# One copy for the values, and ScalarE for some normalisations, in an attention and feed-forward layer on eight cores

## The chip, the cores and the metric

The kernel runs on the 8 cores of one Trainium2 chip. Each core computes one of the 8 sequences of the batch by itself, with no exchange between cores, so all cores run the same program on data of the same size. The time is the device time of the slowest core, in microseconds (us). Engines are named as the profile names them: PE is TensorE (PEld its loads of the stationary operand), DVE VectorE, ACT ScalarE, POOL GpSimd, SP SyncE.

## What is computed

One transformer layer with normalisation behind each part, on x of shape (8, 2048, 1024), with 16 heads of 64. The attention weights are the second-order polynomial 1 + s + s*s/2 in place of an exponential, causal, divided by their sum. The second matmul takes its input as integers, scaled by the largest magnitude of each row, and weights in int8.

```python
def attention(x):                      # per sequence, T = 2048, 16 heads of 64
    q, k, v = x @ Wq.T / 8, x @ Wk.T, x @ Wv.T
    s = einsum('bhqd,bhkd->bhqk', q, k)
    attn = where(causal, 1.0 + s + 0.5 * s * s, 0.0)
    o = einsum('bhqk,bhkd->bhqd', attn, v) / (attn.sum(-1) + 1e-6)
    return o @ Wo.T

def ffn(x):
    x_scale = maximum(abs(x).max(-1), 1e-6) / 127
    x_q = clip(round(x / x_scale), -128, 127)
    return (x_q @ weight_q.T) * x_scale * weight_scale + bias

x = layernorm(x + attention(x))
x = layernorm(x + ffn(x))
```

## The kernel before

**Tiling and stages.** The 2048 rows of a sequence are 16 tiles of 128, and 4 blocks of 512 queries. Attention runs over five groups of queries (`GROUPS`): blocks 0 to 2, and the two halves of block 3. In a group the 8 pairs of heads follow one another. For each step of a pair, PE computes the scores of both heads into one of two PSUM tensors `ps` (L521), ACT turns them into (s/sqrt2 + 1/sqrt2) squared in fp16 (L533), DVE puts the causal mask on the diagonal tiles (L540), and three steps later PE multiplies by the values into `oab` (L577). The missing 0.5 of the polynomial comes from sums of the values over key blocks (`block_sums`, L403 to L416, and L560).

**The values in SBUF.** `vx` holds, for each tile of 128 keys, 8 pairs of heads at a pitch of 130 columns (`VB`): 64 columns of the first head, two columns of ones, 64 of the second head. The stationary operand of L577 is a window of 128 columns. The first head's begins at the pair's first column: its rows 0 to 63 of the product are the output and row 64 is the sum of the weights. The second head's begins two columns later: its output is in rows 64 to 127 and the sum in row 62 (and 63). A projection of values for half the heads fills a PSUM bank of 512 columns, and `place_v` copies it into `vx` by two DVE instructions of 256 columns (L351, L352), one for the first and one for the second heads.

**What else PE does.** Between the steps of attention PE gets filler work, in an order written out by hand for each group (`orders`): K, Q and V are projections for the next block, S block sums, a the output projection of a tile, t its transposes, f the second matmul; T, X, O, W, R and C are loads. In the second group (block 1) the list has a0 to a3, t0 to t3 and f0 to f3, in the third a4 to a7 and so on. The first four tiles thus pass through normalisation, integers, transposes and second matmul within some 80 us. All this filler work shares two PSUM banks `fb` (`take()`), given out in turn: a matmul can begin only when the bank's last reader is done, and that reader is mostly DVE.

**The planner.** Each engine executes its instructions in the order in which they are emitted. Small work is not emitted at once: `at(delay, fn)` gives it a due time on a clock that the program estimates while it emits PE's work, and `when_idle(rank, fn)` puts it into a queue that is taken from by one item when a bank has been read (`evicted()`) or when some time has passed. `run_until(cond)` makes pending items come out until the condition holds.

**The way of a tile.** `out_proj` adds the residual (L740), then the row's largest and smallest value are found (L747, L750) and its sum of squares (ACT, L761). For two tiles at once `chain1` computes mean and variance, `root` the square root on ACT (L783), `scales` seven small DVE instructions (L788 to L794). `quantize` then queues `integers` for each tile, one DVE instruction of 128x1024 (L810) that writes x*S2 + MM2 in fp16 into `xq`. `turn` transposes them on PE (L823), ACT copies them to SBUF (L834), DVE prepares x with the bias (L842). `ffn` runs the second matmul (L289), scales it in PSUM (L864) and adds it (L868). ACT makes the sum of squares (L875). `chain2` and its `root` (L894) find the variance, and `final` takes the reciprocal (L900) and normalises the tile in place by one DVE instruction of 128x1024 (L902), after which the tile goes out by DMA. Tiles 14 and 15 have code of their own at the end.

Of the kernel before, what the change touches and what calls it, by code (L numbers as in the profile page):

```python
# [48 lines left out]
VB = 130  # L49
# [68 lines left out]
def build_nc():  # L118
# [89 lines left out]

    P.op("vector", lambda e: e.memset(consts[:, 0:1], RSQRT2), inc=False)
    P.op("vector", lambda e: e.memset(consts[:, 1:2], EPS_LN), inc=False)  # L210
    vx_ones = vx[:, :].rearrange("p (b g) -> p b g", g=VB)[:, :, 64:66]
    P.op("vector", lambda e: e.memset(ones[:, :], 1.0), inc=False)
    t_const = P.op("vector", lambda e: e.memset(vx_ones, 1.0))

# [131 lines left out]

    def place_v(c, tt, half, bk, bi, tok):
        base = (c * 4 + tt) * VROW + half * 4 * VB
        dst = vx[:, base: base + 4 * VB].rearrange("p (q g) -> p q g", g=VB)
        src = bk[:, :].rearrange("p (q a d) -> p q a d", a=2, d=64)  # L350
        P.op("vector", lambda e: e.tensor_copy(dst[:, :, 0:64], src[:, :, 0, :]), [tok], inc=False)  # L351
        tok = P.op("vector", lambda e: e.tensor_copy(dst[:, :, 66:130], src[:, :, 1, :]))  # L352
        evac_v[(c, tt, half)] = tok
        bank["free"][bi] = tok
        evicted()
# [140 lines left out]
    def attention(grp):  # L496
# [51 lines left out]
        def outputs(p, i, n, subs, cols, diag, g):  # L548
            u = ub[g % NU]
            run_until(lambda: g in t_u)  # L550
            waits = [t_u[g]]
            at_ab = place_of(p)
            banks = at_ab[2]

            final = grp * NP + p == len(GROUPS) * NP - 1
            if i == 0:
                for ab in range(2):
                    base = p * VB + ab * 2

                    t_oconst[c] = P.op("tensor", lambda e, ab=ab, base=base: e.matmul(  # L560
                        oab[:, at_ab[ab]: at_ab[ab] + width], bs[c % 2][:, base: base + 128],
                        step[:, first:first + width], start=(ab == 0 or width == 512), stop=False),
                        [t_oev[at_ab[ab] // 512], t_bs[c], t_const])
            if final and i == 0:
                t = P.op("vector", lambda e: e.tensor_copy(
                    bsz[:, :], bs[c % 2][:, 64:65].broadcast_to([128, 128])), [t_bs[c]])
                zbank.extend(take())
                for ab in range(2):
                    P.op("tensor", lambda e, ab=ab: e.matmul(
                        zbank[0][:, ab * 256: ab * 256 + width], bsz[:, :], step[:, first:first + width],  # L570
                        start=(ab == 0), stop=False), [t, zbank[2]], inc=False)
            for k, (kt, qo, w, col) in enumerate(subs):
                end = i == n - 1 and k == len(subs) - 1
                for ab in range(2):
                    base = kt * VROW + p * VB + ab * 2
                    last = ab == 1 and k == len(subs) - 1
                    tok = P.op("tensor", lambda e, base=base, qo=qo, w=w, col=col, ab=ab, end=end: e.matmul(  # L577
                        oab[:, at_ab[ab] + qo: at_ab[ab] + qo + w],
                        vx[:, base: base + 128],
                        u[:, ab * 512 + col: ab * 512 + col + w],  # L580
                        start=False, stop=(end and (ab == 1 or width == 512))),
                        waits + [evac_v[(kt // 4, kt % 4, p // 4)]], inc=last)
                    waits = []
                    if final:
                        tok = P.op("tensor", lambda e, qo=qo, w=w, col=col, ab=ab, end=end: e.matmul(
                            zbank[0][:, ab * 256 + qo: ab * 256 + qo + w], ones[:, :],
                            u[:, ab * 512 + col: ab * 512 + col + w],
                            start=False, stop=(end and ab == 1)), [], inc=last)
            t_o[g] = tok
            if i == n - 1:  # L590
                if final:
                    finish_last(grp * NP + p, p, tok)
                else:
                    finish(grp * NP + p, p, tok)
# [26 lines left out]
        def finish(k, p, tok):  # L621
# [16 lines left out]
            else:  # L638
# [2 lines left out]
            P.dma("sync", lambda e: e.dma_start(zg[b][0:32, 0:w32], osb[b][64:65, 0:width]),  # L641
                  sem_zg[b], [ta, before])
            tz = P.dma("sync", lambda e: e.dma_start(
                zg[b][32:64, 0:w32], osb[b][62:63, width:2 * width]), sem_zg[b], [tb])
            moved = []

            def move():
# [154 lines left out]
    def quantize():  # L802

        while quant[0] in t_mm2 and (quant[0] < 2 or quant[0] - 2 in t_tr):
# [2 lines left out]

            def integers(k=k):
                buf, _ = home(k)
                t_xq[k] = P.op("vector", lambda e: e.tensor_scalar(  # L810
                    xq[k % 2][:, :], buf[:, :], S2(k, k + 1), MM2(k, k + 1), ALU.mult, ALU.add),
                    [t_mm2[k], t_tr.get(k - 2)])

            when_idle(0, integers)

    def turn(t):
        buf, _ = home(t)
# [65 lines left out]
    def chain2(t0, n):  # L883
# [15 lines left out]
        def final(k, ts):  # L899
            t = V(lambda e: e.reciprocal(D1(k, k + 1), D1(k, k + 1)), [ts])  # L900
            buf, bf = home(k)
            tf = P.op("vector", lambda e: e.tensor_scalar(  # L902
                buf[:, :], buf[:, :], M1(k, k + 1), D1(k, k + 1), ALU.subtract, ALU.mult), [t])
            t_out[k] = P.dma("sync", lambda e: e.dma_start(
                d_out[k * 128:(k + 1) * 128, :], buf[:, :]), sem_ou[bf], [tf])

# [341 lines left out]
```

How the kernel before makes its waits and increments, by code:

```python
        def play(eng, todo):  # L102
            for waits, fn, sem, k in todo:
                for s, v in waits:
                    eng.wait_ge(s.h, v)
                inst = fn(eng)
                if sem is not None:
                    inst.then_inc(sem.h, k)
```

## Time and profile before

| | us |
|---|---|
| median of 3 runs | 623.24 (621.19 to 623.88) |
| profiled execution | 621.77 |
| its span on the slowest core (core 7) | 620.2 |
| spans of the 8 cores | 615.7 to 620.2 |

| engine | busy, us | share of the span |
|---|---|---|
| PE | 568.6 | 92% |
| PEld | 240.5 | 39% |
| DVE | 349.5 | 56% |
| ACT | 369.0 | 59% |
| POOL | 100.1 | 16% |

The profile is one execution, seen on its slowest core; the span runs from that core's first to its last instruction. Busy times of matmuls are modelled, so a busy PE isn't PE at its peak. The granted clock is the share of full speed that the chip gave PE. Idle time of an engine counts only where another waits for it.

### The profile page before, as it was taken

The numbers are of one execution on the slowest core, as the hardware profiler recorded it, in microseconds if no ns is written. First come the engines' busy times: TensorE is split into PE (matmuls) and PEld (weight loads), VectorE is DVE, ScalarE is ACT, GpSimd is POOL, SyncE is SP. The second block draws the span as 40 slices with busy tenths as digits, with TensorE's granted clock in tenths as the row PEclk, the third lists the DMA queues.
The fourth block names the chain that finished last, engine by engine and source line by source line (L and its number), as shares of the span: only waits on it lengthen the run. The fifth ranks groups of instructions, "written<-read, shape, count | busy, mean of one in ns | idle before, by whom it ended". The sixth has DMA issues, their size and how long they took to land.

```text
span 620.2 us, 10434 instructions; the slowest of 8 cores (615.7 to 620.2 us)
## 1 busy us (share of the span) xinstructions
PE 568.6 (92%) x3326; PEld 240.5 (39%) x3326; DVE 349.5 (56%) x784; ACT 369.0 (59%) x419; POOL 100.1 (16%) x147
## 2 busy tenths in 40 slices
PE   1899999999988799999998999999999899889982
PEld 0344444443333233333333333344454444444530
DVE  0226456744578667622776755552677744744586
ACT  0000444435557456466777888767889698889433
POOL 9200222125121102232110000111001100000100
PEclk9999999999999899999999999999999999989988
DMA  8999496739822216688220012323001330002201
GB/s 96 160 159 147 68 150 102 141 109 186 214 63 59 44 27 141 153 150 194 46 42 27 27 35 70 109 89 99 27 15 27 107 132 27 15 15 85 90 1 69
DMA packets 34277, 54.54 MB, mean 88 GB/s; under 512 B 10736, under 2 KB 13616, under 8 KB 34224
## 3 DMA queue, kind: packets, MB, share of 16 engines
q0 software_dynamic: 14976, 31.46, 28.5%
q1 hardware_dynamic: 19248, 22.41, 12.3%
q8 instruction: 28, 0.46, 0.3%
q14 instruction: 25, 0.20, 0.1%
HBM read 61.00 MB, written 8.52 MB: 112 GB/s over the span
## 4 chain that ended last, share of the span: by engine, by line
PE 73%; DVE 11%; issue 5%; DMA 4%; ACT 3%; SPq 1%; POOL 0%; DVEq 0%; POOLq 0%; ACTq 0%
PE fb L289 32%; PE oab L577 19%; PE ps L521 13%; PE oab L560 3%; DMA slot<-xT 2%; ACT u L533 2%; PE ps L365 1%; PE ps L289 1%; PE ps L381 1%; DMA zg<-osb 1%; DVE fb L864 1%; PE oab L289 1%; DVE vx L352 1%; DMA rzb<-zscr 1%; PE fb L403 1%
## 5 line engine op out<-in xcount | busy, mean ns | idle before, releaser
L533 ACT ACTIVATE u<-ps,consts 128x1024 f16<-128x1024 f32 (+2 forms) x288 | 303.4, 1067 | 142.3 <-PE ps L521 139.9
L577 PE MATMUL oab<-u,vx 128*128 128x256 f16 (+3 forms) x864 | 171.2, 305 | 0.0
L521 PE MATMUL ps<-qT,kT 64*128 64x256 f16 (+3 forms) x864 | 110.2, 306 | 2.3 <-ACT u L533 2.0
L540 DVE SCALAR_TENSOR_TENSOR u<-u,cst_sb 128x256 f16<-128x256 f16 (+1 forms) x88 | 55.6, 633 | 75.5 <-ACT u L533 75.1
L577 PEld LDWEIGHTS oab<-u,vx 128*128 128x128 f16 x864 | 62.8, 98 | 59.5 <-issue 45.5
L669 POOL TENSOR_TENSOR slot<-osb,rzb 128x512 f16<-128x512 f32 (+1 forms) x35 | 38.8, 1109 | 280.7 <-DMA rzb<-zscr 255.6
L521 PEld LDWEIGHTS ps<-qT,kT 64*128 64x128 f16 x864 | 30.5, 94 | 120.8 <-issue 119.9
L289 PE MATMUL fb<-wf_sb,xqT 128*128 128x512 f16 x224 | 64.3, 394 | 6.6 <-DVE vx L352 3.2
L289 PE MATMUL fb<-slot,wr 128*128 128x512 f16 x256 | 66.8, 379 | 1.7 <-DVE zg L652 0.8
L289 PE MATMUL fb<-wo_sb,slot 128*128 128x512 f16 x224 | 60.7, 379 | 2.0 <-DVE vx L352 1.9
L289 PE MATMUL fb<-wv_sb,slot 128*128 128x512 f16 x192 | 49.1, 379 | 0.8 <-DVE x L868 0.8
L533 ACT ACT_TABLE_LOAD x1 | 1.3, 1283 | 65.0 <-PE ps L521 65.0
L289 PEld LDWEIGHTS fb<-slot,wr 128*128 128x128 f16 x256 | 24.1, 98 | 27.2 <-issue 4.7
L289 PEld LDWEIGHTS fb<-wf_sb,xqT 128*128 128x128 f16 x224 | 21.7, 100 | 23.6 <-issue 9.8
L322 DVE CAST kT<-fb 128x512 f16<-128x512 f32 x26 | 17.9, 688 | 20.6 <-PE fb L289 20.4
L289 PEld LDWEIGHTS fb<-wo_sb,slot 128*128 128x128 f16 x224 | 21.8, 98 | 18.7 <-issue 3.4
L289 PEld LDWEIGHTS fb<-wv_sb,slot 128*128 128x128 f16 x192 | 18.6, 98 | 21.7 <-issue 1.2
L636 DVE COPY osb<-oab 128x512 f32<-128x512 f32 x20 | 13.8, 689 | 21.7 <-PE oab L577 21.7
L365 PE MATMUL ps<-slot,wk_sb 128*128 128x512 f16 x32 | 11.1, 515 | 15.9 <-DMA slot<-xT 15.9
L864 DVE SCALAR_TENSOR_TENSOR fb<-fb,stat,wsb_sb 128x512 f32<-128x512 f32 x28 | 21.1, 754 | 7.8 <-PE fb L289 7.7
L224 POOL DMA_DIRECT2D slot<-xT x16 | 9.1, 619 | 83.3 <-PE ps L521 49.0
L740 DVE SCALAR_TENSOR_TENSOR x<-fb,x 128x512 f32<-128x512 f32 x24 | 16.5, 686 | 10.5 <-PE fb L289 10.5
(183 smaller groups left out, 586.3 us busy)
## 6 DMA issues: line engine op xcount, KB each, us to landing
rzb<-zscr SPq DMA_DIRECT2D x48, 128.0 KB, 3.3
x<-x_tok POOLq DMA_DIRECT2D x12, 512.0 KB, 7.2
out<-x SPq DMA_DIRECT2D x12, 512.0 KB, 3.2
slot<-xT POOLq DMA_DIRECT2D x16, 256.0 KB, 8.1
wr<-wk POOLq DMA_DIRECT2D x16, 256.0 KB, 5.6
wr<-wq POOLq DMA_DIRECT2D x16, 256.0 KB, 6.2
osb<-osb SPq DMA_DIRECT2D x20, 128.0 KB, 2.3
wk_sb<-wk POOLq DMA_DIRECT2D x8, 256.0 KB, 16.6
```

Source lines behind the costliest of these rows:

```text
L289: tok = P.op("tensor", lambda e, lhs=lhs, rhs=rhs, i=i: e.matmul(out, lhs, rhs, start=(i == 0), stop=(i == n - 1)), list(w) + (list(waits) ...
L322: tok = P.op("vector", lambda e: e.tensor_copy(dst, bk[:, :]), [box[0]])
L365: tok = P.op("tensor", lambda e, fi=fi, p=p, bk=bk: e.matmul(bk, wk[:, p * D + fi * 128: p * D + (fi + 1) * 128], xs(c, fi), start=(fi == ...
L521: tok = P.op("tensor", lambda e, r=r, kt=kt, qo=qo, w=w, col=col, ab=ab: e.matmul(pt[:, ab * 512 + col: ab * 512 + col + w], kT[r:r + 64, ...
L533: tok = P.op("scalar", lambda e: e.activation(dst, src, AF.Square, bias=c_rs, scale=RSQRT2), [t_s[g], t_o.get(g - NU), t_const])
L540: t_u[g] = P.op("vector", lambda e: e.scalar_tensor_tensor(ud, ud, 0.5, tri2[:, None, 0:diag].broadcast_to([128, 2, diag]), ALU.add, ALU.m ...
L560: t_oconst[c] = P.op("tensor", lambda e, ab=ab, base=base: e.matmul(oab[:, at_ab[ab]: at_ab[ab] + width], bs[c % 2][:, base: base + 128], ...
L577: tok = P.op("tensor", lambda e, base=base, qo=qo, w=w, col=col, ab=ab, end=end: e.matmul(oab[:, at_ab[ab] + qo: at_ab[ab] + qo + w], vx[: ...
L636: tb = t_oev[1] = P.op("vector", lambda e: e.tensor_copy(osb[b][:, 512:1024], oab[:, 512:1024]), [tok, before])
L669: t_norm[k] = P.op("gpsimd", lambda e: e.tensor_tensor(slot[o_slot[c]][:, p * 512 + first: p * 512 + first + width], osb[b][:, 0:width], r ...
L740: tok = P.op("vector", lambda e, bk=bk, xh=xh, acc=acc: e.scalar_tensor_tensor(xh, bk, 1.0, xh, ALU.mult, ALU.add, accum_out=acc), [box[0] ...
L864: t1 = P.op("vector", lambda e, bk=bk, half=half: e.scalar_tensor_tensor(bk, bk, XS(t, t + 1), wsb[:, half * 512:(half + 1) * 512], ALU.mu ...
```

## The change

1. The values: the layout becomes 64 columns of a head and one column of ones, for each of the 16 heads (65 columns, the pair still 130). `place_v` is one DVE copy of 512 columns. The second head's window begins one column after the pair's first instead of two, and its sum stands in row 63 only, from where the small DMA of the sums now reads. The memset of the ones follows the new layout. Sizes, counts of matmuls and of DMAs stay.
2. The integers of tiles 0 to 3 are one ACT instruction (identity with scale and bias from columns), emitted 1.8 us after the scales by `at`, no longer through the idle queue.
3. The last normalisation of tiles 0 to 7 is one ACT instruction; ahead of it DVE computes the bias column, minus mean times reciprocal, by one small instruction.

```diff
@@ -208,7 +208,7 @@
 
     P.op("vector", lambda e: e.memset(consts[:, 0:1], RSQRT2), inc=False)
     P.op("vector", lambda e: e.memset(consts[:, 1:2], EPS_LN), inc=False)
-    vx_ones = vx[:, :].rearrange("p (b g) -> p b g", g=VB)[:, :, 64:66]
+    vx_ones = vx[:, :].rearrange("p (h g) -> p h g", g=VB // 2)[:, :, 64:65]
     P.op("vector", lambda e: e.memset(ones[:, :], 1.0), inc=False)
     t_const = P.op("vector", lambda e: e.memset(vx_ones, 1.0))
 
@@ -346,10 +346,9 @@
 
     def place_v(c, tt, half, bk, bi, tok):
         base = (c * 4 + tt) * VROW + half * 4 * VB
-        dst = vx[:, base: base + 4 * VB].rearrange("p (q g) -> p q g", g=VB)
-        src = bk[:, :].rearrange("p (q a d) -> p q a d", a=2, d=64)
-        P.op("vector", lambda e: e.tensor_copy(dst[:, :, 0:64], src[:, :, 0, :]), [tok], inc=False)
-        tok = P.op("vector", lambda e: e.tensor_copy(dst[:, :, 66:130], src[:, :, 1, :]))
+        dst = vx[:, base: base + 4 * VB].rearrange("p (h g) -> p h g", g=VB // 2)[:, :, 0:64]
+        src = bk[:, :].rearrange("p (h d) -> p h d", d=64)
+        tok = P.op("vector", lambda e: e.tensor_copy(dst, src), [tok])
         evac_v[(c, tt, half)] = tok
         bank["free"][bi] = tok
         evicted()
@@ -555,7 +554,7 @@
             final = grp * NP + p == len(GROUPS) * NP - 1
             if i == 0:
                 for ab in range(2):
-                    base = p * VB + ab * 2
+                    base = p * VB + ab
 
                     t_oconst[c] = P.op("tensor", lambda e, ab=ab, base=base: e.matmul(
                         oab[:, at_ab[ab]: at_ab[ab] + width], bs[c % 2][:, base: base + 128],
@@ -572,7 +571,7 @@
             for k, (kt, qo, w, col) in enumerate(subs):
                 end = i == n - 1 and k == len(subs) - 1
                 for ab in range(2):
-                    base = kt * VROW + p * VB + ab * 2
+                    base = kt * VROW + p * VB + ab
                     last = ab == 1 and k == len(subs) - 1
                     tok = P.op("tensor", lambda e, base=base, qo=qo, w=w, col=col, ab=ab, end=end: e.matmul(
                         oab[:, at_ab[ab] + qo: at_ab[ab] + qo + w],
@@ -641,7 +640,7 @@
             P.dma("sync", lambda e: e.dma_start(zg[b][0:32, 0:w32], osb[b][64:65, 0:width]),
                   sem_zg[b], [ta, before])
             tz = P.dma("sync", lambda e: e.dma_start(
-                zg[b][32:64, 0:w32], osb[b][62:63, width:2 * width]), sem_zg[b], [tb])
+                zg[b][32:64, 0:w32], osb[b][63:64, width:2 * width]), sem_zg[b], [tb])
             moved = []
 
             def move():
@@ -807,11 +806,19 @@
 
             def integers(k=k):
                 buf, _ = home(k)
+                if k < 4:
+                    t_xq[k] = P.op("scalar", lambda e: e.activation(
+                        xq[k % 2][:, :], buf[:, :], AF.Identity, bias=MM2(k, k + 1), scale=S2(k, k + 1)),
+                        [t_mm2[k], t_tr.get(k - 2)])
+                    return
                 t_xq[k] = P.op("vector", lambda e: e.tensor_scalar(
                     xq[k % 2][:, :], buf[:, :], S2(k, k + 1), MM2(k, k + 1), ALU.mult, ALU.add),
                     [t_mm2[k], t_tr.get(k - 2)])
 
-            when_idle(0, integers)
+            if k < 4:
+                at(1.8, integers)
+            else:
+                when_idle(0, integers)
 
     def turn(t):
         buf, _ = home(t)
@@ -899,8 +906,15 @@
         def final(k, ts):
             t = V(lambda e: e.reciprocal(D1(k, k + 1), D1(k, k + 1)), [ts])
             buf, bf = home(k)
-            tf = P.op("vector", lambda e: e.tensor_scalar(
-                buf[:, :], buf[:, :], M1(k, k + 1), D1(k, k + 1), ALU.subtract, ALU.mult), [t])
+            if k < 8:
+
+                tb = V(lambda e: e.scalar_tensor_tensor(
+                    MSQ(k, k + 1), M1(k, k + 1), -1.0, D1(k, k + 1), ALU.mult, ALU.mult), [t])
+                tf = P.op("scalar", lambda e: e.activation(
+                    buf[:, :], buf[:, :], AF.Identity, bias=MSQ(k, k + 1), scale=D1(k, k + 1)), [tb])
+            else:
+                tf = P.op("vector", lambda e: e.tensor_scalar(
+                    buf[:, :], buf[:, :], M1(k, k + 1), D1(k, k + 1), ALU.subtract, ALU.mult), [t])
             t_out[k] = P.dma("sync", lambda e: e.dma_start(
                 d_out[k * 128:(k + 1) * 128, :], buf[:, :]), sem_ou[bf], [tf])
```

## Rows read from the trace of the kernel before

**Rows 1.** Busy times: busy us (share of the span) and instructions.

```profile
PE 568.6 (92%) x3326; PEld 240.5 (39%) x3326; DVE 349.5 (56%) x784; ACT 369.0 (59%) x419; POOL 100.1 (16%) x147
```

**Rows 2.** Waits of PE, whole span: us in total, times, longest.

```profile
PE fb L289 <- DVE vx L352: 5.1, 5, 1.6
PE fb L823 <- DVE x L868: 4.1, 2, 2.4
...
PE ps L521 <- ACT u L533: 2.0, 4, 1.2
```

**Rows 3.** Window 210 to 220, cores 1 and 7: length, busy us by engine, clock.

```profile
core 1: us, PE busy (x) PEld busy (x) DVE busy (x) ACT busy (x) POOL busy (x), PEclk, DMA share, GB/s
210.00:220.00 10.00, 7.18 (x34) 2.84 (x34) 5.73 (x10) 4.77 (x6) 1.26 (x1) 0.83 0.16 34
...
core 7: us, PE busy (x) PEld busy (x) DVE busy (x) ACT busy (x) POOL busy (x), PEclk, DMA share, GB/s
210.00:220.00 10.00, 7.55 (x31) 2.95 (x32) 5.15 (x10) 4.53 (x6) 1.26 (x1) 0.66 0.13 35
```

**Rows 4.** Cores: span, mean granted clock.

```profile
core 1: 619.9 us, clock 0.984
...
core 7: 620.2 us, clock 0.981
```

**Rows 5.** Timeline, all engines, 209 to 214: start, length, engine, line, idle before.

```profile
209.04 0.81 DVE L810 TENSOR_SCALAR xq<-x,stat 128x1024 f16<-128x1024 f32 x1
209.77 0.75 DVE L864 SCALAR_TENSOR_TENSOR fb<-fb,stat,wsb_sb 128x512 f32<-128x512 f32 x1
210.63 0.69 DVE L868 SCALAR_TENSOR_TENSOR x<-fb,x 128x512 f32<-128x512 f32 x1
...
211.47 1.01 PE L823 MATMUL fb<-cst_sb,xq 128*128 128x128 f16 x8 [2.41 <-DVE x L868]
211.48 1.06 ACT L875 ACTIVATE junk<-x 128x1024 int8<-128x1024 f32 x1 [2.17 <-DVE x L868]
...
212.57 0.41 DVE L351 CAST vx<-fb 128x256 f16<-128x256 f32 x1
212.91 0.41 DVE L352 CAST vx<-fb 128x256 f16<-128x256 f32 x1
...
213.47 1.01 PE L289 MATMUL fb<-wf_sb,xqT 128*128 128x512 f16 x2 [0.98 <-DVE vx L352]
```

**Rows 6.** DVE by line and shape: busy us, mean ns, idle before.

```profile
L322 DVE CAST kT<-fb 128x512 f16<-128x512 f32 x26 | 17.9, 688 | 20.6 <-PE fb L289 20.4
...
L352 DVE CAST vx<-fb 128x256 f16<-128x256 f32 x26 | 10.7, 413 | 0.0
...
L810 DVE TENSOR_SCALAR xq<-x,stat 128x1024 f16<-128x1024 f32 x12 | 9.6, 809 | 0.3
```

**Rows 7.** Stationary loads and value matmuls, by line and shape.

```profile
L577 PEld LDWEIGHTS oab<-u,vx 128*128 128x128 f16 x864 | 62.8, 98 | 59.5 <-issue 45.5
...
L577 PE MATMUL oab<-u,vx 128*128 128x256 f16 x496 | 82.3, 278 | 0.0
```

**Rows 8.** ACT by line and shape.

```profile
L875 ACT ACTIVATE junk<-x 128x1024 int8<-128x1024 f32 x12 | 12.7, 1054 | 2.9 <-DVE x L868 2.8
...
L1136 ACT ACTIVATE junk<-x1l 128x512 int8<-128x512 f32 x4 | 2.5, 630 | 4.5 <-DVE x1l L1132 3.3 <-DVE stat L1150 1.2
...
L1152 ACT ACTIVATE x1l<-x1l,stat 128x512 f32<-128x512 f32 x2 | 1.6, 806 | 0.6 <-DVE stat L1151 0.6
```

**Rows 9.** Timeline, DVE and PE, 233 to 236.

```profile
233.22 0.81 DVE L902 TENSOR_SCALAR x<-x,stat 128x1024 f32<-128x1024 f32 x1
...
235.65 0.82 PE L403 MATMUL fb<-vx,cst_sb 128*128 128x390 f16 x4 [0.30 <-DVE x L868]
```

**Rows 10.** Window 360 to 380, core 7.

```profile
360.00:380.00 20.00, 19.44 (x102) 7.18 (x100) 11.28 (x27) 16.61 (x20) 1.31 (x1) 1.00 0.22 74
```

**Rows 11.** Two windows of 4 us, core 7.

```profile
196.00:200.00 4.00, 2.51 (x18) 1.21 (x16) 3.11 (x9) 3.35 (x5) 0.59 (x1) 1.00 0.19 58
208.00:212.00 4.00, 1.59 (x12) 0.87 (x11) 3.65 (x10) 1.64 (x2) 0.00 (x0) 0.93 0.54 69
```

## The prediction

> **What bounds the kernel now.** I read the busy times first, then who TensorE (PE) waited for, then the clock and the cores, and last the timeline around the longest wait. PE is busy for 92% of the span [rows 1] while ScalarE (ACT) is at 59%, so the end is set by PE's work, its holes and its clock. In the list of PE's waits the holes of the steady part are nearly all put down to VectorE (DVE): 5.1 us in 5 waits end with L352, the second half of a value copy, and 4.1 us in 2 waits with L868; ACT's squares end only 2.0 us in 4 waits [rows 2]. So the kernel is PE-bound with small holes made by DVE, in the stages where output projection, transposes and the last matmul run beside attention. The worst hole is at 209 to 213.5 us. There the granted clock falls to its lower level, 1.2 of 2.4 GHz: over 210 to 220 us core 1 averages 0.83 and core 7 0.66 [rows 3], so 1.7 and 3.4 us of full-speed work are lost (10 us times 0.17 and 0.34). All eight cores show one or the other of these figures within 0.04. The slowest cores are core 7 with 620.2 us and core 1 with 619.9 [rows 4]. The profiled execution took 621.77 us: this span and 1.57 us around it. The median of the runs is 623.24, so 1.47 above the profiled one; I make the sum on the spans and take the difference off the median.
>
> The timeline shows how the hole comes about [rows 5]. PE has nothing from 209.06 until the transposes of tile 2 at 211.47, 2.41 us. They need a PSUM bank that L868 frees, and DVE, before it does L864 and L868 for that bank, writes the integers of tile 2 (L810 at 209.04). Then come the integers of tile 3, a mask and the value copy, and the next matmul waits 0.98 us more for that copy's bank.
>
> **The value copy.** 64 copies of 128x256 become 32 of 128x512. A half takes 413 ns and a full copy of the same kind from PSUM 688 [rows 6]; the halves start 0.34 us apart [rows 5], so a bank is held for 0.34 + 0.41 = 0.75 us now and 0.69 after. That is 0.06 us for each of the five waits that end there, -0.3 us; between 0 (the new 65-column pitch costs what is saved) and 5 x (2 x 0.41 - 0.69) = -0.65. Elsewhere PE doesn't wait for these copies and the saving is hidden. The column of ones sits at 64 of each 65 and the second head's window starts one column later, so its softmax sum is row 63; the DMAs are as many and as large as before. The trace shows no stationary load that starts at an odd column, which every second head's now does. The nearest row is that of the same loads at even columns, 98 ns [rows 7]; I take 0 for the difference, since windows that already start at steps of 130 columns cost nothing that I can see; the upper bound is a rival below. The memset writes as many ones.
>
> **The integers of tiles 0 to 3.** DVE loses four instructions of 810 ns [rows 6]. Behind those of tiles 0 and 1, some 20 us earlier, PE waits for nothing that they delay: worth nothing. Those of tiles 2 and 3 stand in the hole. L864 starts 0.73 us after L810 did [rows 5], so taking two off brings the value copy forward by 2 x 0.73 = 1.46 us, unless ACT is late. The same on ACT: a 128x512 activation with scale and bias from columns takes 806 ns, and 512 further columns cost 1054 - 630 = 424 [rows 8], so 1.23 us. ACT is idle from 209.31 to 211.48 and then does the sum of squares of tile 0 (L875), which waited for L868 [rows 5]. Queued ahead of that sum, tile 2's integers end at 209.31 + 1.23 = 210.54, and the bank is free at 210.63 + 0.69 - 0.73 = 210.6; the transposes start near 210.6. Then the value copy ends near 211.8 instead of 213.3, and the sum on ACT comes after the integers of tile 3, near 211.8, with nobody waiting for it soon. Term: -1.46, between 0 (ACT late by as much) and -3.39 (both holes close). The order on ACT is written out by the planner: the integers are due 1.8 us after the scales whatever DVE does, so that an ACT instruction stands waiting for L794. Behind it are the attention squares, and behind these the masks on DVE. PE's scores are two squares ahead, which here is over 2 us, so I charge nothing.
>
> **The last normalisation of tiles 0 to 7.** Each takes 0.81 us off DVE [rows 9], adds a one-column instruction there (0.2 us with its gap) and 1.23 us on ACT. For tiles 0 and 1 the DVE work ends just before a bank is freed; PE waits 0.30 us for it at 235.65 [rows 9]: -0.3 (0 to -0.5). Tiles 4 to 7 lie after 360 us, where PE loses nothing to these instructions, and ACT is busy for 16.61 of 20 us [rows 10]. Each insertion delays two or three squares; 20 - 16.61 = 3.39 us hold two insertions (2.5 us), but with less than 1 us left. I charge +0.3 in all, between 0 and one stall of the longest kind seen, 1.2 us [rows 2]. The output DMA leaves up to 1 us later; the load that reuses its buffer is tens of us away from its first reader.
>
> A rule that speaks against this part: by the Trainium skill, "Advanced Engine Details and Errata", section "The Read-Write Bubble", ScalarE is closer to PSUM and VectorE to SBUF, to be used accordingly; these twelve tiles are SBUF to SBUF. The trace agrees (806 ns on ACT for 512 columns, 810 on DVE for 1024), which makes the move a loss of 12 x 0.42 = 5 us if ACT set the end; as ACT has room, the sum above stands.
>
> **The clock.** With PE idle for about 1.9 instead of 3.4 us between 209 and 213.5, the fall may not come. PE was busy for 1.59 of 4 us where the clock fell, and for 2.51 of 4 at 196 to 200 us, where it stayed [rows 11]. After the change I get 1.06 before 209.06 (as now) and 1.2 after 210.6, 2.2 of 4: nearer to the row that held. By the Trainium skill, "TensorE: Matmul & The Clock Gate", section "What's actually happening", the default state is throttled and activity releases it, which fits a fall in the least active stretch.
>
> Sum without the clock: -0.3 - 1.46 - 0.3 + 0.3 = -1.8 us. With it the slowest core changes: core 7 gets 620.2 - 1.8 - 3.4 = 615.0, core 1 619.9 - 1.8 - 1.7 = 616.4. The slowest is then 616.4, or -3.8.
>
> **The rivals.**
> A, the forecast: relief and held clock, 623.24 - 3.8 = 619.4.
> B: relief, but the clock falls all the same: 623.24 - 1.8 = 621.4. For it: PE still idles 1.5 us in one piece there.
> C: nothing arrives. The value copy costs the same in the new pitch, and what DVE saves is waited for on ACT, whose integers take 1.23 instead of 0.81 us and come in pairs: 623.2.
> D, slower: ACT runs its queue in order, and the integers of tile 2 stand behind the sum of squares that waits for L868. Then that sum runs at 210.6 to 211.8, the integers to 213.0, and the transposes start 1.5 us later than now, not 0.9 earlier; PE idles 3.9 us in one piece, and the cores with the short fall (1.7 us) get the long one (3.4) or a second. 1.5 + 0.7 for the same in later pairs + 1.7 = +3.9: 627.1. It decides from the point where the integers' due time is later than that sum's. Against it: the sum is due 1.8 us after the eviction, which DVE does after the scales, and the integers are due 1.8 us after the scales.
> E, slower: odd-column loads cost twice. The matmul of 256 columns is some 107 ns at full clock (256 / 2.4), a load 98; at 196 ns each of the 248 loads of odd heads before such matmuls (half of 496) [rows 7] would show 89 ns, +22 us: 645.
> F: the planner places other work differently once its idle slots are free, and a new hole eats the gain: 622 to 625.
>
> **How the numbers follow.** A 0.42, B 0.22, C 0.12, D 0.13, E 0.04, F 0.07. About 0.5%, 3.1 us, can be told from no change, so faster means below 620.1. Most of A and the lower tail of B (larger bounds of the integers' term) give 0.45; slower is D, E and a bit of F, 0.18; the rest, 0.37, is within. The range reaches from 615.0 (A with both holes closed: -3.39 instead of -1.46, -0.65 and -0.5 for the copy and the finals, and a later fall of the clock gone too) to 627.0, the edge of D; below, above and in E about 0.15 is left out.
>
> **What would show it.** The value copy has one row of about 0.69 us and the odd loads 98 ns. The integers of tile 2 on ACT end before L868 does, the PE wait before the transposes of tile 2 is about 1.5 us and the one before the next matmul nearly gone, and the clock at 210 to 220 us is near 1.00 on all cores. At 360 to 400 us ACT is over 90% busy in some stretch and PE's waits for the squares are a few tenths. Wrong would be: a new PE wait on ACT near 209 us (D), or on ACT's squares over 1.2 us at 370 to 395; or the fall still there with the hole halved (B).

## The result, and the profile after

The changed kernel takes 625.57 us (median of 9 runs) where the kernel before takes 623.08 (9 runs beside it): a ratio of 1.0052, with a 95% interval from 1.0036 to 1.0068. It is 0.5% slower, 3.2 us by the ratio. All ratios and means of this document leave out the few executions in which cores of a die were held to a lower clock (here one, of 675.2 us), so they are not quotients of the medians. Predicted were 619.4 us, faster, with a range of 615.0 to 627.0. The number lies in the range, and the sign is wrong.

The busy times of the changed kernel (busy us, share of the span, instructions), to be read against [rows 1]:

```profile
span 624.0 us, 10419 instructions; the slowest of 8 cores (616.4 to 624.0 us)
...
PE 567.4 (91%) x3326; PEld 240.5 (39%) x3326; DVE 339.6 (54%) x748; ACT 381.1 (61%) x431; POOL 99.8 (16%) x147
```

DVE has lost 10 us of busy time and ACT has gained 12, and each instruction costs what was forecast. These are groups of instructions by line and shape, of the changed kernel (busy us, mean ns of one, idle time before them and what ended it); the first answers to [rows 6], the second to [rows 7]:

```profile
L351 DVE CAST vx<-fb 128x512 f16<-128x512 f32 x26 | 17.8, 687 | 2.2 <-PE fb L289 2.1
...
L576 PEld LDWEIGHTS oab<-u,vx 128*128 128x128 f16 x864 | 63.0, 98 | 59.3 <-issue 45.6
...
L913 ACT ACTIVATE x<-x,stat 128x1024 f32<-128x1024 f32 x8 | 9.9, 1236 | 6.7 <-DVE stat L911 3.8 <-DVE stat L907 2.7
L810 ACT ACTIVATE xq<-x,stat 128x1024 f16<-128x1024 f32 x4 | 4.7, 1231 | 1.6 <-DVE stat L793 1.6
```

The value copy takes 687 ns, a load 98 ns (half of the loads start at odd columns), an ACT instruction 1.23 us. What matters stands at the end of the third line: ahead of the eight normalisations on ACT (L913) the engine stood idle for 6.7 us and waited for DVE (L911, L907).

Who PE waited for, over the span of the slowest core, against [rows 2] (us in total, times, longest):

```profile
PE fb L289 <- DVE vx L351: 7.1, 6, 2.2
PE ps L520 <- ACT u L532: 6.9, 9, 1.7
PE fb L830 <- DVE x L875: 3.4, 2, 1.7
```

The waits before the transposes fell from 4.1 to 3.4 us. The waits for ACT's squares rose from 2.0 to 6.9 us and those for the value copy from 5.1 to 7.1.

The totals don't say where in the kernel this happens. PE executes the same 3326 matmuls in the same order in both kernels, so one can subtract the start of each matmul in one profile from its start in the other, counting the matmuls in order of start, and average over the 8 cores. A step in that difference is time lost or won at that place. Differences of up to 0.7 us by matmul 700 (159 us) come from the loads at the start and vary from run to run. The first line is the time of that matmul in the kernel before, the others are us later (+) or earlier (-) than it:

```
matmul number              700    836    850    960   1100   1700   1840   3325
time in the kernel before  159.0  187.9  191.3  217.3  246.3  366.0  393.9  606.3
changed kernel             -0.5   +0.4   +1.5   -1.5   -0.6   -0.4   +2.5   +2.9
```

The forecast gain is there: between matmuls 850 and 960 the kernel wins 3.0 us. But it has lost 0.9 us by matmul 836, exactly 1.1 us between 836 and 850 (on each of the 8 cores), loses 0.9 us in 217 to 246 us and 2.9 us in 366 to 394 us. The runs below take these places one by one.

### The profile page after: what moved, and what is told of

Read it like the earlier page. It is cut to its first block, busy times and chain, and to the rows that moved or that the text cites. A ratio compares the mean times of both kernels' runs of the same rounds, so it can differ in the third digit from the quotient of the medians.

```text
span 624.0 us, 10419 instructions; the slowest of 8 cores (616.4 to 624.0 us)
## 1 busy us (share of the span) xinstructions
PE 567.4 (91%) x3326; PEld 240.5 (39%) x3326; DVE 339.6 (54%) x748; ACT 381.1 (61%) x431; POOL 99.8 (16%) x147
## 4 chain that ended last, share of the span: by engine, by line
PE 70%; DVE 11%; issue 6%; ACT 5%; DMA 5%; POOL 1%; DVEq 0%; ACTq 0%; POOLq 0%
PE fb L289 31%; PE oab L576 19%; PE ps L520 13%; DMA wv_sb<-wv 5%; ACT u L532 3%; PE oab L559 3%; DVE vx L351 1%; DVE fb L871 1%; PE ps L289 1%; DVE x L875 1%; POOL wk_sb L231 1%; PE fb L402 1%; PE oab L380 1%; PE fb L380 1%; DVE osb L638 1%
## 5 line engine op out<-in xcount | busy, mean ns | idle before, releaser
L539 DVE SCALAR_TENSOR_TENSOR u<-u,cst_sb 128x256 f16<-128x256 f16 (+1 forms) x88 | 57.2, 650 | 82.6 <-ACT u L532 82.2
L289 PE MATMUL fb<-wf_sb,xqT 128*128 128x512 f16 x224 | 63.0, 388 | 6.4 <-DVE vx L351 2.7
L289 PE MATMUL fb<-wo_sb,slot 128*128 128x512 f16 x224 | 62.4, 388 | 4.5 <-DVE vx L351 4.5
L871 DVE SCALAR_TENSOR_TENSOR fb<-fb,stat,wsb_sb 128x512 f32<-128x512 f32 x28 | 21.1, 754 | 6.6 <-PE fb L289 6.5
L327 DVE TENSOR_SCALAR qT<-fb 128x512 f16<-128x512 f32 x26 | 17.8, 683 | 7.8 <-PE fb L289 7.5
```

Of the source, the lines that this page charges most:

```text
L289: tok = P.op("tensor", lambda e, lhs=lhs, rhs=rhs, i=i: e.matmul(out, lhs, rhs, start=(i == 0), stop=(i == n - 1)), list(w) + (list(waits) ...
L327: tok = P.op("vector", lambda e: e.tensor_scalar(dst, bk[:, :], QSCALE, None, ALU.mult), [box[0], t_slast.get(c * NP + p - QRING)])
L539: t_u[g] = P.op("vector", lambda e: e.scalar_tensor_tensor(ud, ud, 0.5, tri2[:, None, 0:diag].broadcast_to([128, 2, diag]), ALU.add, ALU.m ...
L871: t1 = P.op("vector", lambda e, bk=bk, half=half: e.scalar_tensor_tensor(bk, bk, XS(t, t + 1), wsb[:, half * 512:(half + 1) * 512], ALU.mu ...
```

## Experiments

All medians stand beside runs of the kernel before on the same chip, whose own median was between 622.1 and 622.7 us; so the ratio decides, not the median. With each run goes its line of the table above.

**The three parts alone.** Each of these kernels is the kernel before with one part of the change.

The value copy and its layout alone:

```diff
-            if k < 8:      (final on ScalarE)
+            if k < 0:
-                if k < 4:  (integers on ScalarE)
+                if k < 0:
```

> The new layout and the single value copy alone; integers and last normalisations stay on DVE. Theory Q (ScalarE's own queue order costs the time: its new instructions wait for DVE or stand ahead of the attention squares): no change or up to 0.5 us less than the kernel before, 622.6 to 623.1, and the loads of the stationary values stay at 98 ns. Rival L (the odd columns or the 65-column pitch cost time): 1 to 3 us slower than before.

Measured 622.45 us, ratio 1.0012 (0.9999 to 1.0025), so no change that can be told. The mean over all 8 cores, which varies less than the slowest core, is 618.2 us in both kernels, with a 95% interval of 0.3 us on the difference. The loads stay at 98 ns; neither the layout nor the odd columns cost anything that can be measured in the total.

```
e1_copy_only               -0.7   +0.2   +0.1   -0.2   -0.1   -0.1   -0.1   +0.3
```

The profiled execution has one step, +0.9 us by matmul 836, where I expected a small gain. It is the wait for the value copy near 179 us, 1.87 us on seven of the eight cores before and 2.17 on six now. Its timeline in the kernel with the copy alone, core 0 (start, length, engine, line, idle before; L777 here is L778 of the kernel before):

```profile
177.45 0.15 DVE L777 TENSOR_TENSOR stat<-stat 128x2 f32<-128x2 f32 x1
178.06 0.16 DVE L778 TENSOR_TENSOR stat<-stat 128x2 f32<-128x2 f32 x1 [0.46 <-DVE stat L777]
178.33 0.16 DVE L779 TENSOR_TENSOR stat<-stat 128x2 f32<-128x2 f32 x1
178.43 0.69 DVE L351 CAST vx<-fb 128x512 f16<-128x512 f32 x1
179.27 1.89 PE L289 MATMUL fb<-wo_sb,slot 128*128 128x512 f16 x8 [2.17 <-DVE vx L351]
```

and in the kernel before, core 0:

```profile
178.22 0.15 DVE L778 TENSOR_TENSOR stat<-stat 128x2 f32<-128x2 f32 x1
178.47 0.16 DVE L779 TENSOR_TENSOR stat<-stat 128x2 f32<-128x2 f32 x1
178.84 0.42 DVE L351 CAST vx<-fb 128x256 f16<-128x256 f32 x1
179.18 0.41 DVE L352 CAST vx<-fb 128x256 f16<-128x256 f32 x1
179.74 1.89 PE L289 MATMUL fb<-wo_sb,slot 128*128 128x512 f16 x8 [1.88 <-DVE vx L352]
```

The copy is shorter by 0.06 us, as computed (0.69 instead of 0.34 + 0.41), but two small DVE instructions of 160 ns that follow each other every 0.25 us stand 0.61 us apart in the new kernel, with nothing that the profile shows between them. That is 0.36 us, more than the copy saves. All eight cores of all five kernels with the single copy show this gap at the same instruction, and no core of the seven kernels with two copies does. By the count in the last section it hangs on the place in DVE's stream of instructions, not on the instruction; what the engine does there stays open. The rest of the step is the clock: of the eight cores, four average 0.89 over 176 to 192 us in this kernel and none in the kernel before. Which cores fall varies between executions; over all profiled ones it is 16 of 40 cores with the single copy and 5 of 56 without.

The integers of tiles 0 to 3 alone:

```diff
-                t_xq[k] = P.op("vector", lambda e: e.tensor_scalar(...), ...)
+                if k < 4:
+                    t_xq[k] = P.op("scalar", lambda e: e.activation(...), ...)
-            when_idle(0, integers)
+            if k < 4:
+                at(1.8, integers)
```

> The integers of tiles 0 to 3 alone on ScalarE, old value layout, normalisations on DVE. Theory Q: the hole at 209 to 213 us shrinks by about 1.5 us and its clock loss of 1.7 to 3.4 us may go; against it about 1.1 us appear near 192 us, where the squares stand behind the pair of integers of tiles 0 and 1 and the value copy behind their mask. Net 1 to 3 us faster than before, 620 to 622. Rival (the integers are what makes the change slow): 625 or more.

Measured 620.73 us, ratio 0.9974 (0.9963 to 0.9986): faster by 1.6 us, as expected. Both places show:

```
e2_ints_only               -0.7   -1.0   +0.2   -2.5   -2.6   -2.4   -2.4   -2.0
```

+1.1 us between matmuls 836 and 850, again the same on all cores, and -2.7 us between 850 and 960.

The last normalisation of tiles 0 to 7 alone:

```diff
-            tf = P.op("vector", lambda e: e.tensor_scalar(...), [t])
+            if k < 8:
+                tb = V(lambda e: e.scalar_tensor_tensor(...), [t])
+                tf = P.op("scalar", lambda e: e.activation(...), [tb])
```

> The last normalisation of tiles 0 to 7 alone on ScalarE. Theory Q: ScalarE stands waiting for the bias column that DVE makes behind two readings of a bank, and the squares behind it are late; waits of PE for the squares of 0.8 us near 235 and together 3 us between 370 and 400 us. Net 3 to 4 us slower than before, 626 to 627, more than the whole change. Rival (these stalls come from the copy or the integers): within 1 us of before.

Measured 625.84 us, ratio 1.0066 (1.0047 to 1.0086): this part alone is slower than the whole change.

```
e3_finals_only             +0.1   +0.0   +0.0   +0.2   +1.0   +1.1   +3.9   +4.4
```

+0.8 us where tiles 0 and 1 are normalised and +2.8 us where tiles 4 to 7 are. The mechanism can be read in the changed kernel's timeline, core 7, around tile 5:

```profile
371.41 1.10 ACT L532 ACTIVATE u<-ps,consts 128x1024 f16<-128x1024 f32 x1
...
372.23 0.28 PE L520 MATMUL ps<-qT,kT 64*128 64x256 f16 x2
...
373.41 0.39 PE L520 MATMUL ps<-qT,kT 64*128 64x128 f16 x4
...
373.82 0.69 DVE L875 SCALAR_TENSOR_TENSOR x<-fb,x 128x512 f32<-128x512 f32 x1
...
374.43 0.16 DVE L907 RECIPROCAL stat<-stat 128x1 f32<-128x1 f32 x1
374.70 0.16 DVE L911 SCALAR_TENSOR_TENSOR stat<-stat 128x1 f32<-128x1 f32 x1
374.95 1.24 ACT L913 ACTIVATE x<-x,stat 128x1024 f32<-128x1024 f32 x1 [2.44 <-DVE stat L911]
376.10 1.67 ACT L532 ACTIVATE u<-ps,consts 128x512 f16<-128x512 f32 x2
...
376.91 0.39 PE L520 MATMUL ps<-qT,kT 64*128 64x512 f16 x2 [1.70 <-ACT u L532]
```

ACT is done with a square at 372.51. The next instruction in its queue is the normalisation, and this needs a column that DVE makes behind the two readings of a PSUM bank (L871, L875). So ACT stands still for 2.44 us and then works for 1.24. The two squares behind it could have begun soon after 372.2 and 373.4, when their scores came; they begin at 376.1, and PE, two scores further on, waits 1.70 us. At 395.07 the same happens with 1.20 us of idle time and a PE wait of 1.40, and at 232.38 with 2.70 and 0.81.

**Wait or work?** ACT is busy for 33.0 of 40 us between 364 and 404, so a rival explanation was that 1.23 us more for each tile are simply too much. Three kernels separate the two. First the whole change, with ACT's instruction, and the output DMA behind it, placed later:

```diff
-                tf = P.op("scalar", lambda e: e.activation(...), [tb])
+                def on_act():
+                    tf = P.op("scalar", lambda e: e.activation(...), [tb])
+                    t_out[k] = P.dma("sync", ...)
+                at(2.5, on_act)
+                return
```

> The whole change, but ScalarE's normalisation (and its output DMA) is placed 2.5 us later by the planner than the DVE instructions that it needs, so that it no longer stands waiting for them; ScalarE does the same work. Theory Q (the wait in the queue costs, not the work): ScalarE's idle time ended by DVE ahead of the normalisations falls from 2.7, 2.4 and 1.2 us to near 0, PE's waits for the squares between 370 and 400 us fall from 3.1 us to under 1; 3 us faster than the changed kernel, about 622.5. Rival O (ScalarE is too full there, 1.23 us more for each tile is too much wherever it stands): same as the changed kernel, 625 to 626.

Measured 620.65 us, ratio to before 0.9983 (0.9969 to 0.9997); the changed kernel stands at 1.0052, so this edit is worth 0.7%, over 4 us.

```
e4_finals_later            -0.0   +0.5   +1.6   -1.8   -2.2   -1.9   -1.9   -1.3
```

The step of +2.9 us between matmuls 1700 and 1840 is gone, and so is the one of +0.9 before 1100. In the order of ACT's instructions the normalisations have moved behind one or two squares; the orders of PE, DVE and POOL are the same. These are all that is left of ACT's waits in front of the normalisations in the whole span, and of PE's waits between 364 and 404 us, in this kernel (core 1, its slowest):

```profile
ACT x L915 <- DVE stat L907: 0.5, 1, 0.5
```

```profile
PE oab L559 <- ACT osb L634: 0.2, 1, 0.2
```

Then the wait alone. The kernel before keeps its normalisation on DVE and gets a one-column instruction on ACT that waits for the same reciprocal:

```diff
             t = V(lambda e: e.reciprocal(D1(k, k + 1), D1(k, k + 1)), [ts])
+            if k < 8:
+                P.op("scalar", lambda e: e.activation(MSQ(k, k + 1), D1(k, k + 1), AF.Identity), [t])
```

> The kernel before, with one added ScalarE instruction of one column for each of tiles 0 to 7, at the place where the change puts the last normalisation, waiting for the same reciprocal of DVE. Its result is not used; the normalisation itself stays on DVE. Theory Q (the wait in the in-order queue costs): PE's waits for the squares between 364 and 404 us are 1 to 2.5 us (3.1 us with the whole normalisation there, since the 1.2 us of work still comes on top of the wait), total 1 to 3 us slower than before. Rival O (only the 1.2 us of work costs): same as before, within 0.3 us, as 0.3 us of small work vanish in the gaps.

Measured 625.24 us, ratio 1.0039 (1.0023 to 1.0054).

```
e5_wait_alone              +0.3   +0.5   +0.5   +0.4   +0.5   +0.6   +1.7   +2.2
```

An instruction of 0.2 us costs PE 1.1 us between matmuls 1700 and 1840, on every core. ACT on core 5:

```profile
374.80 0.20 ACT L903 ACTIVATE stat<-stat 128x1 f32<-128x1 f32 x1 [2.17 <-DVE stat L900]
...
394.23 0.20 ACT L903 ACTIVATE stat<-stat 128x1 f32<-128x1 f32 x1 [2.86 <-DVE stat L900]
```

The total rises by more than that: 0.3 us stem from the start and 0.5 from between 500 and 554 us, where nothing was edited. And the work alone, eight instructions of the same size, emitted at the same places, that wait for nothing of DVE:

```diff
+            if k < 8:
+                t_junk[0] = P.op("scalar", lambda e: e.activation(
+                    junk[:, :], wsb[:, :], AF.Identity, bias=c_eps, scale=c_rs), [tok_c["wsb"], t_junk[0]])
```

> The kernel before, with an added ScalarE instruction of 128x1024 with scale and bias columns (some 1.23 us) for each of tiles 0 to 7 at the same places, reading a constant tensor and waiting for nothing of DVE; its result is not used, the normalisation stays on DVE. Theory Q: PE's waits for the squares between 364 and 404 us stay under 0.5 us and the time is within 0.5 us of before. Rival O (the work costs): the 3 us of the finals come back, 625 to 626.

Measured 623.04 us, ratio 1.0013 (0.9999 to 1.0027).

```
e6_work_alone              +0.3   +0.3   +0.3   +0.4   +0.2   +0.3   +0.3   +0.3
```

No step of more than 0.1 us behind the start, though between 364 and 404 us ACT is busier here (35.16 us) than in the changed kernel (33.0). The added instructions and that window on core 5 (length, then busy us of PE, PEld, DVE, ACT and POOL, the clock):

```profile
L903 ACT ACTIVATE junk<-wsb_sb,consts 128x1024 int8<-128x1024 f32 x8 | 9.9, 1235 | 0.1
```

```profile
364.00:404.00 40.00, 39.44 (x202) 14.14 (x200) 22.36 (x55) 35.16 (x41) 3.68 (x3) 1.00 0.25 80
```

So between matmuls 1700 and 1840 the work alone costs under 0.1 us, the wait alone 1.1 and both together 2.8 (the finals alone) to 2.9 (the whole change). The parts don't add up: together they cost 1.7 us more than apart. The reading that fits is that the wait uses up the lead that ACT has over PE, and only then does the work cost: two stalls, each with 1.24 us of work behind it, could cost up to 2.5 us more. No run shows this lead by itself.

**The pair of integers of tiles 0 and 1.** Where the changed kernel loses 1.1 us, ACT does two integers in a row, then the sum of squares of a tile, and only then the squares of attention. Changed kernel, core 7:

```profile
187.41 2.36 ACT L810 ACTIVATE xq<-x,stat 128x1024 f16<-128x1024 f32 x2
...
189.67 1.04 ACT L760 ACTIVATE junk<-x 128x1024 int8<-128x1024 f32 x1
...
190.71 1.67 ACT L532 ACTIVATE u<-ps,consts 128x512 f16<-128x512 f32 x2
...
191.48 0.42 DVE L539 SCALAR_TENSOR_TENSOR u<-u,cst_sb 128x256 f16<-128x256 f16 x1 [1.90 <-ACT u L532]
191.82 0.69 DVE L351 CAST vx<-fb 128x512 f16<-128x512 f32 x1
...
192.66 0.59 PE L289 MATMUL fb<-wo_sb,slot 128*128 128x512 f16 x2 [1.19 <-DVE vx L351]
```

A mask on DVE waits 1.90 us for the late square, the value copy stands behind the mask, and PE waits 1.19 us for the bank of the value copy. Two ways out were tried, both without the other parts. Only the integers of tiles 2 and 3 on ACT:

```diff
-                if k < 4:
+                if k in (2, 3):
```

> Only the integers of tiles 2 and 3 on ScalarE, all else as before. Theory: the pair of tiles 0 and 1 costs about 1.1 us near 192 us (squares behind it, the mask and the value copy behind these) and gains nothing, that of tiles 2 and 3 gains 1.5 us and the clock. So 1 us faster than with all four, 619.5 to 620, 3 us under before. Rival (the pair of tiles 0 and 1 is neutral, as I predicted): the same as with all four, 620.7.

Measured 620.17 us, ratio 0.9975 (0.9957 to 0.9992).

```
e7_ints_2_3                +0.3   +0.9   +0.9   -2.0   -1.7   -1.7   -1.7   -1.7
```

The trace confirms the place, +0.0 between 836 and 850 instead of +1.1, and the total doesn't confirm the gain: it is the same as with all four. By the mean over all cores it is 2.1 us under the kernel before (interval 0.4 on either side), with all four 1.6 (0.4): a difference of 0.5 us, give or take 0.6, where 1.1 were expected. In the profiled execution two cores have a clock of 0.89 over 176 to 192 us, ahead of all that the edit moves, and three one of 0.91 over 206 to 224 us. Second, all four on ACT, but those of the odd tile later, so that a square comes between them:

```diff
-                at(1.8, integers)
+                at(1.8 if k % 2 == 0 else 4.4, integers)
```

> Only the integers of tiles 0 to 3 on ScalarE, as in the run with the integers alone, but those of the odd tile placed 2.6 us later than those of the even one, so that a pair no longer stands ahead of the squares. Theory: the new wait of 1.1 to 1.25 us near 191 us goes, PE gets 1.1 us back there by the trace; the total falls by up to 1 us, to 619.7 to 620.7. Rival (the wait near 191 us comes from the value copy standing behind the sum of squares L761 and its mask, whatever the pair does): it stays at 1.1 us.

Measured 619.48 us, ratio 0.9952 (0.9935 to 0.9968), the lowest ratio here: 0.5% under the kernel before, and 1.0% under the change as it was made (0.9952 / 1.0052). By the mean over all cores it is 3.2 us under the kernel before (0.4 on either side), against 1.6 with the pairs together. Its interval overlaps those of the kernel with tiles 2 and 3 alone and of the two below.

```
e9_ints_apart              +0.2   +0.0   +0.0   -3.2   -3.2   -3.1   -3.1   -2.9
```

ACT's order there, on core 2:

```profile
187.35 1.23 ACT L811 ACTIVATE xq<-x,stat 128x1024 f16<-128x1024 f32 x1
188.48 1.05 ACT L761 ACTIVATE junk<-x 128x1024 int8<-128x1024 f32 x1
...
189.52 0.67 ACT L533 ACTIVATE u<-ps,consts 128x512 f16<-128x512 f32 x1
190.09 1.24 ACT L811 ACTIVATE xq<-x,stat 128x1024 f16<-128x1024 f32 x1
```

The same instructions cost nothing at this place once one square goes between them, on each of the 8 cores.

**All parts, mended.** Later normalisations with the integers of tiles 2 and 3 alone, and later normalisations with the integers set apart:

> The changed kernel with the normalisations on ScalarE placed 2.5 us later and only the integers of tiles 2 and 3 on ScalarE. Theory: 1 us faster than with the later normalisations alone, 619.6, and no more than 0.5 us apart from the integers of tiles 2 and 3 alone, since neither the copy nor the normalisations are waited for by PE. Rival (the relief of DVE by the eight normalisations is worth something by itself once ScalarE doesn't wait): 618.5 or less.

> The whole changed kernel with both mends: normalisations on ScalarE 2.5 us later, integers of the odd tile 2.6 us after those of the even one. Theory: PE ahead of the changed kernel by 1.1 us from 191 us on and by 4 us from 400 us on; 619.5 to 620.7, the best or within 0.5 us of the best. Rival (the mends only move the waits): 622 or more.

Measured 620.28 us, ratio 0.9961 (0.9944 to 0.9977), and 620.53 us, ratio 0.9958 (0.9932 to 0.9984).

```
e8_all_mended              +0.1   +1.5   +1.4   -1.8   -2.6   -2.5   -2.4   -1.3
e10_apart_later            -0.3   +0.7   +0.6   -2.4   -2.8   -2.6   -2.5   -2.0
```

The change as a whole thus works with two due times corrected, and is 0.9% faster than as it was made. It isn't faster than the integers set apart alone. In the profiled executions of the three kernels with later normalisations, what DVE saves by them is worth 0.4 to 0.8 us between matmuls 960 and 1100 and nothing at tiles 4 to 7, and 0.5 to 1.3 us are lost near 179 us, 0.3 by the longer wait and most of the rest by the clock.

## Why the prediction was wrong

**What bounds the kernel: right.** PE with its holes made by DVE. The gain came where the holes were.

**The value copy: right in its mechanism, and the gain didn't come.** Forecast were -0.3 us for five waits. The 0.06 us a copy are real: the copy alone gains them between matmuls 836 and 850 on each of the 8 cores. But the gap near 178 us costs 0.36 us, and in the profiled execution, with the clock behind it, the copy alone shows +0.9 us between matmuls 700 and 836. The total shows neither gain nor loss (618.2 us against 618.2 on the mean of the cores), so whether the copy costs anything by itself stays open. The gap was in no row of before, and my range for the term ended at 0, without a reason for excluding a loss.

**The integers of tiles 2 and 3: right, in place and size.** Forecast were -1.46 us and up to 3.4 us by the clock. The changed kernel, core 7, has at this place (against [rows 5]):

```profile
210.63 2.37 ACT L810 ACTIVATE xq<-x,stat 128x1024 f16<-128x1024 f32 x2 [1.59 <-DVE stat L793]
210.81 0.75 DVE L871 SCALAR_TENSOR_TENSOR fb<-fb,stat,wsb_sb 128x512 f32<-128x512 f32 x1
211.67 0.69 DVE L875 SCALAR_TENSOR_TENSOR x<-fb,x 128x512 f32<-128x512 f32 x1
...
212.62 0.61 PE L830 MATMUL fb<-cst_sb,xq 128*128 128x128 f16 x8 [1.67 <-DVE x L875]
...
213.72 0.59 PE L289 MATMUL fb<-wf_sb,xqT 128*128 128x512 f16 x2 [0.49 <-DVE vx L351]
```

The waits are 1.67 and 0.49 us instead of 2.41 and 0.98: 1.23 us less, where I had 1.46. Here too ACT waits for DVE (1.59 us), and here it costs nothing, because PE itself stands still. The clock over 210 to 220 us (against [rows 3]) is 1.00 on five cores and 0.83 on the three others; the worst core before had 0.66. With the clock, PE wins 2.2 to 4.0 us by core, 3.0 on average, where the forecast had 3.2 to 4.9. The clock is not luck of one execution: over 206 to 224 us it is 1.00 on 39 of 56 cores in the seven kernels with the integers of tiles 2 and 3 on ACT, and on none of 40 in the five others. By the Trainium skill, "TensorE: Matmul & The Clock Gate", section "What's actually happening", activity releases the throttle. The traces agree: with the waits a third shorter the clock stayed up on most cores. Rival D, which put tile 2's integers behind the sum of squares (L875 in the kernel before, L882 in the changed one), didn't happen here.

**The integers of tiles 0 and 1: wrong.** I wrote that PE waits for nothing that those of DVE delay. That is true of taking them off DVE, and I didn't ask what they delay on ACT. They delay two squares, these a mask, and the mask the value copy: +1.1 us, where the sum had 0. I had named this chain, squares and masks, for the other pair and put nothing down for it.

**The normalisations of tiles 4 to 7: the step that failed and turned the sign.** I charged +0.3 us, between 0 and 1.2, from the share of time that ACT is busy [rows 10]. Measured are +2.9. The share says whether the work fits, and it does: 1.23 us each with no wait cost under 0.1 (the work alone). It doesn't say where the instruction stands when what it needs isn't there. For the integers I had written that an ACT instruction stands waiting for DVE; for the normalisations, where the planner emits ACT's instruction in the same breath as a DVE chain behind an eviction, I didn't. The rows for it were in the trace of before. There, on core 7, the reciprocal that ACT would wait for (L900) stands ahead of L902, behind L864 and L868, and ACT does two squares in the time in which it would have stood waiting:

```profile
372.07 0.75 DVE L864 SCALAR_TENSOR_TENSOR fb<-fb,stat,wsb_sb 128x512 f32<-128x512 f32 x1
372.13 0.69 ACT L533 ACTIVATE u<-ps,consts 128x512 f16<-128x512 f32 x1 [0.50 <-PE ps L521]
372.93 0.69 DVE L868 SCALAR_TENSOR_TENSOR x<-fb,x 128x512 f32<-128x512 f32 x1
...
373.42 1.11 ACT L533 ACTIVATE u<-ps,consts 128x1024 f16<-128x1024 f32 x1 [0.61 <-PE ps L521]
...
373.54 0.16 DVE L900 RECIPROCAL stat<-stat 128x1 f32<-128x1 f32 x1
```

The bound of one stall was wrong too; there are two of them, for tiles 5 and 7. Rivals C and D each had half of this: C had ACT as the place, D the in-order wait, at another instruction.

**The normalisations of tiles 0 and 1**: forecast -0.3, measured +0.9 in the changed kernel and +0.8 alone, by the same wait (2.70 us on ACT, 0.81 on PE); with the wait gone -0.4, which is the term as it was forecast.

**The rule on SBUF and PSUM**: by the Trainium skill, "Advanced Engine Details and Errata", section "The Read-Write Bubble", ScalarE is closer to PSUM and VectorE to SBUF, which speaks against this work on ScalarE. The traces agree: each of these instructions takes 1.23 us there instead of 0.81. But this was not why the change lost: the kernel with the work alone does eight of them in addition at 1.0013 of the time.

**The sum as measured**, by the first table: start -0.5; the copy and its clock +0.9; the first pair of integers +1.1; the second pair with the clock -3.0; tiles 0 and 1 +0.9; tiles 4 to 7 +2.9; the rest +0.5. That is +2.9 us on the average of the cores, before rounding. The slowest core went from 620.2 to 624.0, and the ratio says 3.2. The measured 625.57 us lie in the range of the forecast only because that range reached to the edge of rival D, whose mechanism didn't happen.

## What to carry to other kernels

When an instruction moves to another engine, its length is the smaller question. Ask what it waits for at the moment at which the new engine reaches it, and what stands behind it there: ACT stood idle for 2.44 us before a late operand while the scores for its next two squares came, and so held up PE, which needed them. If the operand comes from an engine that runs behind a plan, emit the consumer later than the producer by that lag; here 2.5 us on the planner's clock turned a loss of 0.5% into a gain of 0.2%. And put no two optional instructions in a row ahead of work that paces another engine.

## What the runs showed of the hardware

- Small DVE instructions can take over 1 us longer beside a POOL instruction. In the kernel before, none of some 1300 DVE instructions on one or two columns with no POOL instruction beside them took over 0.23 us, on any core; 14 took 1.1 to 1.6 us, all of them where POOL multiplies two tensors in SBUF (L669), and they end within 0.1 us of the POOL instruction. One of them, on core 0, is part of the wait near 179 us:

```profile
176.08 1.62 DVE L773 TENSOR_SCALAR stat<-stat 128x2 f32<-128x2 f32 x1
176.38 1.28 POOL L669 TENSOR_TENSOR slot<-osb,rzb 128x512 f16<-128x512 f32 x1
```

- Stationary loads that start at an odd fp16 column take the same 98 ns as those at even ones, and a PSUM copy into rows of 65 fp16 columns the same 687 ns as one into contiguous columns (689).
- A gap of 0.46 us between two small DVE instructions appeared when instructions ahead of it were merged. If one counts all of DVE's instructions in a trace in order of start, those without busy time too, it stands at number 315 (from 0) in all five kernels with the single copy. The other gaps of 0.25 us or more behind the start that no other engine ended stand at 571, 699, 827, 956, 1083, 1211 and 1339, each give or take 2, in the eight kernels that have any: all some 128 or a multiple of it apart. So such a gap comes at fixed places of the stream, and a change that shortens the stream decides which instruction it meets. What the engine does there no run shows.
- After one and the same PE wait of about 2 us the granted clock fell on some cores of an execution and not on others (0.89 over 16 us on three cores of the changed kernel, 1.00 on five; 0.11 times 16 is 1.8 us). Differences of this size between cores can hide a gain of 1 us that is identical on all of them in the trace, which is how the total of the integers of tiles 2 and 3 alone may be read; no run shows it.
